# Cross attention: keys projected in thirds and values in single tiles over nine steps, the split of the keys on GpSimd

## The reference, cut to what matters

```python
xq = _layernorm(result, ln2_g, ln2_b)
xs = _layernorm(src, ln2_g, ln2_b)          # src: 1500 rows of 128 for each batch
kv = xs @ ed_wkv
k2, v2 = (_heads(t) for t in jnp.split(kv, 2, axis=-1))      # 16 heads of 8
q2 = _heads(xq @ ed_wq)
wei2 = jnp.einsum('bhtd,bhjd->bhtj', q2, k2) * scale
wei2 = jax.nn.softmax(wei2, axis=-1)
ed_out = _merge(jnp.einsum('bhtj,bhjd->bhtd', wei2, v2)) @ ed_wproj + ed_bproj
result = result + ed_out
```

## Time and profile before

| | us |
|---|---|
| three executions | 1436.42, 1438.62 (median), 1440.64 |
| the profiled execution | 1435.06 |
| its span | 1433.3 |
| PE busy | 1186.2 (83%) |
| DVE busy | 1008.1 (70%) |
| ACT busy | 744.6 (52%) |
| GpSimd (POOL) busy | 730.5 (51%) |

### The profile page before, as it was taken

One profiled execution on the slowest core, in us unless ns is written; L12 is line 12 of the kernel. 1 busy time (PEld: TensorE's weight loads), 2 busy tenths in 40 slices (PEclk: granted clock), 3 DMA queues, 4 the chain that ended last, 5 costly groups with the idle time before them and its releaser, 6 DMA issues. The chain is left out here.

```text
span 1433.3 us, 38489 instructions
## 1 busy us (share of the span) xinstructions
PE 1186.2 (83%) x15852; PEld 760.5 (53%) x15852; DVE 1008.1 (70%) x1819; ACT 744.6 (52%) x1021; POOL 730.5 (51%) x1047
## 2 busy tenths in 40 slices
PE   3888836898989999999999999897496977869784
PEld 2555523555555555555556565554343746347472
DVE  5677765787888888888888787876456373774733
ACT  2333332567676767666676767675333425234150
POOL 2345648646455555555464646420068394783940
PEclk9999957999999999999999999999987999989995
DMA  7100013232313132313132222110000000000000
GB/s 177 49 0 0 0 33 120 79 100 66 112 59 112 64 109 69 109 56 121 58 99 80 95 83 86 58 49 20 16 0 2 1 7 3 0 6 0 6 0 6
DMA packets 70383, 75.66 MB, mean 53 GB/s; under 512 B 21308, under 2 KB 64956, under 8 KB 70108
## 3 DMA queue, kind: packets, MB, share of 16 engines
q1 hardware_dynamic: 70236, 73.58, 16.7%
HBM read 32.91 MB, written 0.92 MB: 24 GB/s over the span
## 5 line engine op out<-in xcount | busy, mean ns | idle before, releaser
L916 DVE TENSOR_REDUCE tops_sb<-ps_b 112x2 f32<-112x1000 f32 x384 | 460.0, 1198 | 130.2 <-PE ps_b L777 130.0
L878 ACT ACTIVATE probs_sb<-ps_a 128x896 f32<-128x896 f32 x352 | 322.6, 916 | 91.5 <-PE ps_a L758 91.5
L749 PE MATMUL ps_d<-probs_sb,values_sb 128*32 128x112 f32 x6144 | 226.8, 265 | 1.0 <-ACT probs_sb L878 1.0
L777 PE MATMUL ps_b<-keys_sb,queries_sb 64*112 64x500 f16 x768 | 162.6, 419 | 69.2 <-DVE tops_sb L916 63.7
L217 POOL TENSOR_SCALAR context_sb<-context_sb,ln_sb 125x128 f32<-125x128 f32 x384 | 166.4, 450 | 7.9 <-POOL ln_sb L235 7.8
L226 POOL TENSOR_TENSOR ln_sb<-st_sb 125x12 f32<-125x12 f32 x32 | 7.2, 223 | 308.4 <-DVE st_sb L960 283.0
L749 PEld LDWEIGHTS ps_d<-probs_sb,values_sb 128*32 128x32 f32 x6144 | 134.1, 109 | 40.2 <-issue 6.7
L758 PEld LDWEIGHTS ps_a<-queries_sb,keys_sb 64*128 64x128 f16 x3072 | 123.7, 103 | 52.4 <-ACT probs_sb L878 9.0
L777 PEld LDWEIGHTS ps_b<-keys_sb,queries_sb 64*112 64x112 f16 x768 | 49.6, 124 | 186.9 <-DVE tops_sb L916 120.9
L758 PE MATMUL ps_a<-queries_sb,keys_sb 64*128 64x112 f16 x3072 | 139.8, 210 | 6.2 <-ACT probs_sb L878 6.0
L1087 POOL TENSOR_TENSOR turn_b_sb<-turn_b_sb,const_sb 128x512 f32<-128x512 f32 x64 | 83.0, 1297 | 98.0 <-DVE turn_b_sb L1422 98.0
(11 more groups left out here) (253 smaller groups left out, 2019.3 us busy)
## 6 DMA issues: line engine op xcount, KB each, us to landing
keys_sb<-k_split_sb SPq DMA_DIRECT2D x288, 125.0 KB, 3.0
context_sb<-in_ctx SPq DMA_DIRECT2D x32, 750.0 KB
queries_sb<-q_split_sb SPq DMA_DIRECT2D x24, 112.0 KB, 5.5
keys_sb<-in_ones SPq DMA_DIRECT2D x3, 375.0 KB, 4.8
w_qk_sb<-in_w_qkv SPq DMA_DIRECT2D x1, 1024.0 KB, 11.5
queries_sb<-shift_sb SPq DMA_DIRECT2D x64, 1.8 KB
x_all_sb<-in_x SPq DMA_DIRECT2D x2, 448.0 KB
queries_sb<-in_zeros SPq DMA_DIRECT2D x8, 112.0 KB, 5.5
```

Source lines behind the costliest of these rows:

```text
L749: last = nc.tensor.matmul(o_bank[32 * (g % 4):32 * (g % 4) + 32, 112 * (g // 4):112 * (g // 4) + 112], values[r][:, k, g, :], probs[k % 2] ...
L777: last = nc.tensor.matmul(ps_b[0:2 * T, 512 * e:512 * e + 500], queries_of(b + d, e, g), keys[(r + d) % 3][64 * e:64 * e + 64, g, 500 * u: ...
L878: nc.scalar.activation(probs[s % 2][:].rearrange("p (e n) -> p e n", e=2), halves(ps_a[:, :]), ACT.Exp).then_inc(Q["probs_ready"], 1)
L916: nc.vector.tensor_reduce(tops[(b + d) % 2][:, :, n // 3, n % 3], ps_b[0:2 * T, :].rearrange("p (e n) -> p e n", e=2)[:, :, 0:500], axis=A ...
```

## The change

K is projected in nine pieces (three buffers in thirds of 168, 166 and 166 columns, `KEYS_CUT`), placed behind the other PE work of steps 0 to 4; V in twelve single tiles, three behind each of steps 5 to 8. ACT now copies K as it is, in float32, to a new SBUF buffer `k_rows` (two of them), and GpSimd makes the high half (a copy to float16) and the low half (a subtraction) from there. On DVE the subtraction is gone, the statistics come two tiles at a time in steps 2 and 4 to 8, and the output's division and its keeping move from steps 0 and 7 to 1 and 4; PE turns the output back in step 3 instead of 7. GpSimd's iteration becomes: eight tiles of the normalising, split of the first K piece, the other four tiles, the two other splits, sums of b+4, deviation of b+4. The two PSUM buffers alternate over the iterations (`ring_of`), so that the use of one never follows itself.

```diff
--- before.py
+++ after.py
@@ -607,10 +607,13 @@
             UNITS = {**{q: q + 3 for q in range(9)}, 9: 0, 10: 1, 11: 2}
             AHEAD = (9, 10, 11)
             COMBINE, NEG, SHIFT = 9, 9, 10
-            KEYS, VALUES = (1, 2, 3), (4, 5, 6)
-            TURN = (9, 10, 11)
-            STATS, SUM = (4, 5, 6, 7), 11
-            O_TURN, O_BACK = 0, 7
+            KEYS = {0: ((0, 0),), 1: ((0, 1), (0, 2)), 2: ((1, 0), (1, 1)), 3: ((1, 2), (2, 0)), 4: ((2, 1), (2, 2))}
+            VALUES = {5: ((0, 0), (0, 1), (0, 2)), 6: ((0, 3), (1, 0), (1, 1)), 7: ((1, 2), (1, 3), (2, 0)),
+                      8: ((2, 1), (2, 2), (2, 3))}
+            KEYS_OUT, VALUES_OUT, TURN = (1, 3, 4), (6, 7, 8), (9, 10, 11)
+            KEYS_CUT = (0, 168, 334, 500)
+            STATS, SUM = (2, 4, 5, 6, 7, 8), 11
+            O_TURN, O_ROWS, O_BACK, O_KEEP = 0, 1, 3, 4
             PARTS = 4
             W = H0 * T
+            k_rows = [sb2(f"k_rows{n}", [128, 500]) for n in range(2)]
...
+            def ring_of(b, i):
+                return ring[(b + i) % 2]
...
@@ -682,19 +691,31 @@
                     def emit(b, r, has):
                         wait = waiter(pool, b, r)
-                        if has(3) and b + 3 > 0:
-                            wait("st_ready", 3, 1)
-                            wait("z_ready", 2, 3)
-                            context_deviation(pool, b + 3)
+                        norm = has(3) and b + 3 > 0
+                        if norm:
                             wait("stats_ready", 3, 1)
                             wait("sums_ready", 3, 1)
                             alone(pool)
-                            context_normed(r)
+                            context_normed(r, 0, 8)
+                        for u in range(3):
+                            if u == 1 and norm:
+                                context_normed(r, 8, KT)
+                            if has(2):
+                                k_slice = slice(500 * u, 500 * u + 500)
+                                wait("k_read", 2, u + 1)
+                                wait("keys_in", 2, 0)
+                                nc.gpsimd.tensor_copy(k_split[:, 0, k_slice], k_rows[(b + u) % 2][:]).then_inc(Q["khigh_ready"], 1)
+                                wait("khigh_ready", 2, u + 1)
+                                nc.gpsimd.tensor_tensor(k_split[:, 1, k_slice], k_rows[(b + u) % 2][:], k_split[:, 0, k_slice],
+                                                        ALU.subtract).then_inc(Q["klow_ready"], 1)
                         if has(4) and b + 4 > 0:
                             wait("context_in", 4, 16)
                             wait("pool_done", 4, 0)
                             alone(pool)
                             context_sums(pool, b + 4, (r + 1) % 3)
+                            wait("st_ready", 4, 1)
+                            wait("z_ready", 3, 3)
+                            context_deviation(pool, b + 4)
                         if b == -5:
                             nc.gpsimd.memset(xs_t[:, J:JP], 0.0).then_inc(cleared, 1)
...
@@ -781,14 +802,6 @@
                         for s in range(KT):
                             d = 2 if s in AHEAD else 1
-                            if has(2) and s in KEYS:
-                                u = KEYS.index(s)
-                                if u == 0:
-                                    wait("xs_ready", 2, 3)
-                                elif u == 2:
-                                    wait("klow_ready", 2, 1)
-                                nc.tensor.matmul(ring[u % 2][:, 0:500], w_kv[:, 0:128], xs_t[:, 500 * u:500 * u + 500],
-                                                 start=True, stop=True).then_inc(Q["k_done"], 1)
                             if has(d):
                                 scan(UNITS[s], d)
                             if s > 0 and has(0):
@@ -804,17 +817,26 @@
                                 wait("shift_in", 0, 32)
                                 wait("probs_ready", 0, 0)
                                 scores(b, r, s)
-                            if has(2) and s in VALUES:
-                                u = VALUES.index(s)
-                                if u < 2:
-                                    wait("klow_ready", 2, u + 2)
-                                else:
+                            for u, part in KEYS.get(s, ()) if has(2) else ():
+                                if part == 0:
+                                    wait("xs_ready", 2, min(u + 2, 3))
+                                    if u == 2:
+                                        wait("k_read", 2, 1)
+                                lo, hi = KEYS_CUT[part], KEYS_CUT[part + 1]
+                                last = nc.tensor.matmul(ring_of(b, u)[:, lo:hi], w_kv[:, 0:128],
+                                                        xs_t[:, 500 * u + lo:500 * u + hi], start=True, stop=True)
+                                if part == 2:
+                                    last.then_inc(Q["k_done"], 1)
+                            for u, k in VALUES.get(s, ()) if has(2) else ():
+                                if k == 0 and u < 2:
+                                    wait("k_read", 2, u + 2)
+                                elif k == 0:
                                     wait("values_ready", 2, 1)
-                                for k in range(4):
-                                    last = nc.tensor.matmul(ring[1 - u % 2][:, 128 * k:128 * k + 128],
-                                                            xs_t[:, 4 * KEY * u + KEY * k:4 * KEY * u + KEY * k + KEY],
-                                                            w_kv[:, 128:256], start=True, stop=True)
-                                last.then_inc(Q["v_done"], 1)
+                                last = nc.tensor.matmul(ring_of(b, 3 + u)[:, 128 * k:128 * k + 128],
+                                                        xs_t[:, 4 * KEY * u + KEY * k:4 * KEY * u + KEY * k + KEY],
+                                                        w_kv[:, 128:256], start=True, stop=True)
+                                if k == 3:
+                                    last.then_inc(Q["v_done"], 1)
                             if has(3) and s in TURN:
                                 u = TURN.index(s)
...
-                                    last = nc.tensor.transpose(ring[u % 2][:, KP * k:KP * k + KP],
+                                    last = nc.tensor.transpose(ring_of(b, 6 + u)[:, KP * k:KP * k + KP],
...
@@ -866,12 +888,6 @@
                         wait = waiter(act, b, r)
                         r2 = (r + 2) % 3
                         for s in range(KT):
-                            if has(2) and s in KEYS:
-                                u = KEYS.index(s)
-                                wait("k_done", 2, u + 1)
-                                wait("keys_in", 2, 0)
-                                nc.scalar.copy(k_split[:, 0, 500 * u:500 * u + 500], ring[u % 2][:, 0:500]
-                                               ).then_inc(Q["khigh_ready"], 1)
                             if s > 0 and has(0):
                                 wait("scores_done", 0, s + 1)
@@ -888,18 +904,23 @@
                                 wait("pv_done", 0, s - 1)
                                 nc.scalar.activation(probs[s % 2][:].rearrange("p (e n) -> p e n", e=2),
                                                      halves(ps_a[:, :]), ACT.Exp).then_inc(Q["probs_ready"], 1)
-                            if has(2) and s in VALUES:
-                                u = VALUES.index(s)
+                            if has(2) and s in KEYS_OUT:
+                                u = KEYS_OUT.index(s)
+                                wait("k_done", 2, u + 1)
+                                wait("klow_ready", 2, u - 1)
+                                nc.scalar.copy(k_rows[(b + u) % 2][:], ring_of(b, u)[:, 0:500]).then_inc(Q["k_read"], 1)
+                            if has(2) and s in VALUES_OUT:
+                                u = VALUES_OUT.index(s)
                                 wait("v_done", 2, u + 1)
                                 wait("pv_done", -1, KT)
                                 nc.scalar.copy(values[r2][:, 4 * u:4 * u + 4, :, 0:16],
-                                               ring[1 - u % 2].rearrange("p (k g n) -> p k g n", k=4, g=8)
+                                               ring_of(b, 3 + u).rearrange("p (k g n) -> p k g n", k=4, g=8)
                                                ).then_inc(Q["values_ready"], 1)
                             if has(3) and s in TURN:
                                 u = TURN.index(s)
                                 wait("t_done", 3, u + 1)
                                 wait("v_done", 2, u + 1)
-                                nc.scalar.activation(xs_t[:, 500 * u:500 * u + 500], ring[u % 2][:, 0:500], ACT.Identity,
```

(15 more changed lines are left out.)

7 lines of the change are left out of this document (4 added, 3 removed).

## The result

The change took 1393.34 us (median; 1392.48 to 1394.02), the kernel before 1438.46 (1436.42 to 1440.64) beside it: ratio 0.9691, 95% interval 0.9676 to 0.9706. The forecast was 1400 with a range of 1386 to 1430.

The account below looks back on a forecast made before the run. PE was taken to bound six steps of about 2.1 us, the 1.72 us scan loop others. 30 x 1.5 saved, plus 1, minus 8, is 38 us less: 1397 profiled, 1400 median, range 1386 to 1430.

Parts of the forecast that it names:

- The bound: Middle stage: PE bounds six steps of about 2.1 us, the 1.72 us scan loop others; spreading work fills the gaps.
- The sum on PE: PE's steps of one iteration, priced from scan to scan, add up to 22.7 us, 1.5 less than 24.2.
- step 0: First step of an iteration on PE: 2.87 us becomes 2.1, with a third of K replacing the whole K.
- Step 3: PE's step with a K piece and the output's turn back: 2.02 us.
- rival B: Smaller gain: every K piece on PE pays the fixed 0.20 us itself, 23.5 an iteration, 1425 us; chance 0.17.
- The split: GpSimd's copy and subtraction for one K piece: about 2.0 us, bringing its own loop to 20.3, no bound.
- Rival A: Slower: long GpSimd splits make keys late and step 9 waits, 1434 to 1470 us, about 1452; chance 0.12.
- The keys' way round: GpSimd to DMA to step 9's scan: keys land at 15.5, scan at 17.4, hidden with 1.9 us to spare.
- The reordering: GpSimd's deviation leaves the iteration's head, where its 5.2 us would stand ahead of the first split.
- The start: Iteration -2: the first scan waits for keys GpSimd makes, landing at about 238 us, a loss of 8 us.
- rival C: Slower: GpSimd's subtractions delay DVE's statistics pairs by 0.75 us through the shared SBUF port, 1482 us; chance 0.02.

Follow-up runs that it names:

- e2: Changed kernel with K whole ahead of the scans of steps 1 to 3 and V in fours in steps 4 to 6, as before: 1444.47 us.
- e10: Changed kernel with three of the twelve V tiles of each batch computed twice: 1414.2 us, 0.9836 of the kernel before.
- e4: Changed kernel with the output's division back in step 0 and its turn back and keeping back in step 7: 1398.55 us.
- e8: Changed kernel with K in whole matmuls at the end of steps 1, 2 and 3, none in steps 0 and 4: 1415.97 us.
- e6: Changed kernel with one more GpSimd subtraction, into a buffer nobody reads, ahead of all three low halves of K: 1411.6 us.
- e1: Changed kernel with K's split back on ACT (high half) and DVE (low half) from PSUM, statistics in threes: 1381.37 us.
- e7: Changed kernel with only the first batch's K (iteration -2) split by ACT and DVE out of PSUM: 1383.4 us.

## Why the prediction was right, and where not

**The bound: right.** The gaps of the short steps were the reserve, and spreading K and V over the steps filled them. PE is busy for 22.40 of 22.52 us where I had said above 97%, and the waits for DVE are nearly gone. e2 shows that the rest of the change alone wins only 0.1 us an iteration, e10 that PE is now the bound, one to one. One part I had not priced at all: with K and V spread, the output's new places are worth 0.25 us (e4). I wrote that without cover its division would cost "some 0.2 in each of two steps", but not what the old places would cost.

**The sum on PE: right to 0.2 us, step 0 by luck.** Step 0 was forecast at 2.1 and is 2.09, steps 1, 2 and 4 at 1.82 and are 1.83, 1.82 and 1.88, steps 5 to 8 at 1.95 and are 1.93, steps 9 to 11 at 5.33 and are 5.33. Step 3, with the output's turn back, I put at 2.02, and it is 1.84. The turn back stands at the end of step 3, so the rest of its cost is in step 4 (1.88; in e4, where nothing is turned back ahead of it, that step is 1.83). In all it costs some 0.07 where I had 0.2. Together the iteration is 22.52 for 22.7. The price of 0.20 for each group, not for each matmul (rival B), holds: a group of two thirds begins 1.06 behind the scan and ends with the next, 0.77 later.

Step 0 came out at 2.1 because two sizes were wrong in opposite directions. I took 1.03 for the whole K and 0.26 for the third. But without any K step 0 is 2.02 (e8), with a whole one 2.86 (e2) and with the third 2.09: behind the turn the whole K costs 0.84 and the third 0.07. Most of the third runs where PE would wait, and not 0.12 of its 0.38 as I had it. The 0.39 that I read as PE's idle time is the row of the weight load; PE's own row of that turn has 0.26 of waiting for ACT.

**Where the 7 us went by which 1400 was too high.** The 29 iterations between the copies gave 48.5 us, and I had 43.5. By the first copy my terms make a loss of 5.5 (8, less 1 and 1.5 for iterations -1 and 0), and it was 4.3. What lies behind iteration 30, which I had at nothing, took 1.6 longer; the part of it behind the last copy lies anywhere from 409 to 414 us in these profiles, so this is no effect of the change. The last 2 to 3 us are the profiled execution, which I put 3.6 below the median and which was 0.9 below.

**The split: right in size.** 0.60 and 1.13 us, and 719.31 to 721.11 for one split in the rows below, 1.80 for the forecast 2.0. Rival A needed 3.1.

```profile
719.31 0.60 POOL L707 CAST k_split_sb<-k_rows_sb 128x500 f16<-128x500 f32 x1 [1.16 <-ACT k_rows_sb L911]
...
720.00 1.13 POOL L709 TENSOR_TENSOR k_split_sb<-k_rows_sb,k_split_sb 128x500 f16<-128x500 f32 x1
721.11 1.74 POOL L217 TENSOR_SCALAR context_sb<-context_sb,ln_sb 125x128 f32<-125x128 f32 x4
```

GpSimd waits 57.7 us in all for ACT's copy (L707 above), which it can afford.

**The keys' way round: hidden, as I said, but with more to spare.** The term that was mis-sized is the landing: I took 3.0 us, the median over all nine DMAs. The last of them, which counts, lands in about 2.1 (e6), or 2.3 at the start. So 1.9 us to spare are about 3.0.

**The reordering: right result, wrong argument.** I wrote that at its old place the deviation would stand ahead of the first split and that "none of this would fit". In either kernel GpSimd does sums, deviation and normalising of a batch one behind the other, with the same waits; the edit only writes the deviation at the end of one iteration and not at the head of the next. With the split behind the first eight tiles both ways of writing give the same row of instructions, so there was nothing to keep out. What keeps the deviation early is that DVE's statistics end in step 8 and that the split stands behind it. No run put the split ahead of the deviation, so what that would cost stays open.

**The start: right in kind, 8 us forecast, about 6.4 measured.** The first scan moved from 230.01 to 237.20, of which 0.8 us came with the stage before it (its first PE row is at 210.35 for 209.57). The parts were each a little shorter: split and landing. By the first copy of the output only 4.3 of the 7.2 was left, since iterations -1 and 0 are shorter by 1.68 each. What I did not see is the other side of this term: the DVE time that the move frees buys nothing, so the loss could have been left out. I wrote that the subtractions "cost nothing by themselves once PE is the bound", and did not draw the conclusion. e1 and e7 did, by 12 and 10 us in the medians, of which 8 stand ahead of the first copy of the output.

**The shared port (rival C): not there.** The statistics last 279 ns on average in both pages. In the change the pair below lies wholly inside GpSimd's subtraction of 720.00 to 721.13 (above), and lasts 0.47 us like the pair at 731.48, when GpSimd is idle.

```profile
720.14 0.47 DVE L974 BATCH_NORM_STATS2 st_sb<-context_sb 125x6 f32<-125x128 f32 x2
```

The Trainium skill, Perfetto Trace Analysis, section Optimizing Scalar/DVE Operations, warns that moving operations between GpSimd and DVE might not help, because they share an SBUF read port. The move gained nothing here, but not for that reason: neither these statistics nor, in the move back, the split became longer. In e1 DVE's subtraction, reading PSUM, lasted 0.67 us as before, beside GpSimd's sums, and the maximum and the subtraction find room beside each other in a PE step:

```profile
710.96 1.20 DVE L931 TENSOR_REDUCE tops_sb<-ps_b 112x2 f32<-112x1000 f32 x1
...
712.08 0.67 DVE L966 TENSOR_TENSOR k_split_sb<-ps_c,k_split_sb 128x500 f16<-128x500 f32 x1
712.79 1.20 DVE L931 TENSOR_REDUCE tops_sb<-ps_b 112x2 f32<-112x1000 f32 x1
```

The maximum starts at 710.96, the subtraction behind it at 712.08, and the next maximum at 712.79, 1.83 behind the first. The scan waits for the maximum alone, and it comes first.

## What to carry to other kernels

When PE is bound in some steps of a loop and waits for a fixed chain in others, cut its independent work small enough to put the same amount into every step, and price each step from scan to scan before you cut; the saving ends where the last gap does. Relief for an engine that is not the bound was worth nothing here, so ask of each such move what it costs where the pipeline has not filled yet, and give the first iteration its own, shorter path. Where data goes to its reader by a DMA, look at what was issued ahead of it on the same queue.
